# A four-layer spectral mixer on one core: TensorE's waits moved from the head of each unit to the last products of the unit in front

## What is computed

```python
xs = jnp.fft.rfft2(x, axes=(1, 2))                       # 64 x 33 modes
o1 = relu(block_matmul(xs, w1) + b1)                      # 8 blocks of 48 channels, complex
o2 = block_matmul(o1, w2) + b2
out = jnp.fft.irfft2(softshrink(o2, 0.01), s=(64, 64)) + x
```

## Time and profile before

| | |
|---|---|
| median of 3 runs | 995.19 us (990.65 to 997.57) |
| the profiled execution | 993.3 us, of which the span from its first to its last instruction 991.3 us |
| TensorE matmul busy | 916.0 us, 92% |
| VectorE, ScalarE, GpSimd busy | 577.1, 475.8, 81.1 us |
| TensorE's share of the chain that ended last | 82% |
| mean granted clock | 0.976 |

### The profile page before, as it was taken

The page is one execution under the profiler, slowest core; times in us unless marked ns, Lnnn a source line. Parts: engine busy times, 40 slices in busy tenths (PEclk is TensorE's granted clock), DMA queues, the critical chain, the costliest instruction groups (busy, mean ns, idle before and its releaser), DMA issues.

```text
span 991.3 us, 14302 instructions
## 1 busy us (share of the span) xinstructions
PE 916.0 (92%) x5168; PEld 460.3 (46%) x5168; DVE 577.1 (58%) x869; ACT 475.8 (48%) x757; POOL 81.1 (8%) x157
## 2 busy tenths in 40 slices
PE   2799999999999988999999999999999999999933
PEld 1555555665676655444444434444444444444411
DVE  1255555455454765787775676666666666666511
ACT  2455444444545424434343445565655656666521
POOL 3011111011111110000000101000000000000001
PEclk8899999999999999999999999999999999999986
DMA  9879699469648979856143443343654474554463
GB/s 283 324 206 298 202 282 366 150 180 283 248 136 269 260 237 277 210 138 164 48 114 95 112 127 108 108 123 113 213 170 129 153 247 134 161 156 153 142 192 128
DMA packets 95703, 184.41 MB, mean 186 GB/s; under 512 B 13007, under 2 KB 73769, under 8 KB 93842
## 3 DMA queue, kind: packets, MB, share of 16 engines
q1 hardware_dynamic: 85490, 143.65, 48.0%
q0 software_dynamic: 9696, 39.56, 12.4%
q10 hardware_dynamic: 448, 0.30, 0.1%
HBM read 104.32 MB, written 79.14 MB: 185 GB/s over the span
## 4 chain that ended last, share of the span: by engine, by line
PE 82%; DMA 9%; SPq 2%; DVE 2%; ACT 2%; issue 1%; POOL 0%; ACTq 0%; DVEq 0%
PE psum L948 17%; PE psum L957 16%; PE psum L987 8%; PE psum L1041 6%; PE psum L1065 6%; PE psum L1025 6%; DMA RG<-rows_along_h 6%; PE psum L936 5%; PE psum L967 5%; PE psum L998 4%; PE psum L1052 3%; PE psum L913 3%; PE psum L1014 2%; DMA rows_along_h<-RD 1%; SPq L611 1%
## 5 line engine op out<-in xcount | busy, mean ns | idle before, releaser
L1374 DVE SCALAR_TENSOR_TENSOR RA<-psum,RA 112x896 f32<-112x896 f32 (+1 forms) x120 | 124.1, 1035 | 206.3 <-ACT RA L1222 205.9
L1222 ACT ACTIVATE RA<-psum,small 112x896 f32<-112x896 f32 (+1 forms) x120 | 115.7, 964 | 94.7 <-PE psum L957 94.7
L957 PE MATMUL psum<-RA,RW 112*64 112x448 f32 (+1 forms) x640 | 131.1, 531 | 1.4 <-ACT RA L1213 1.4
L1213 ACT ACTIVATE RA<-psum,RW 112x448 f32<-112x448 f32 (+1 forms) x160 | 89.2, 609 | 80.0 <-PE psum L948 80.0
L1334 DVE COPY RD<-psum 128x672 f32<-128x672 f32 (+2 forms) x122 | 69.5, 571 | 58.3 <-PE psum L987 56.8
L987 PE MATMUL psum<-RD,const 128*128 128x384 f32 (+1 forms) x304 | 98.3, 445 | 3.7 <-DVE RD L1334 2.7
L1207 ACT ACTIVATE RA<-psum 128x384 f32<-128x384 f32 (+2 forms) x72 | 50.6, 702 | 78.9 <-PE psum L936 52.6
L936 PE MATMUL psum<-const,RX 128*112 128x128 f32 x528 | 68.5, 282 | 17.1 <-DMA RX<-rows_along_w 17.1
L1359 DVE TENSOR_TENSOR RX<-RX,RA 112x768 f32<-112x768 f32 (+2 forms) x80 | 80.8, 1011 | 2.5
L1207 ACT ACTIVATE RD<-psum 128x384 f32<-128x384 f32 (+2 forms) x122 | 64.0, 525 | 32.9 <-PE psum L987 30.9
L936 PEld LDWEIGHTS psum<-const,RX 128*112 128x112 f32 x528 | 61.2, 180 | 35.7 <-issue 34.9
(11 more groups left out here) (103 smaller groups left out, 1070.1 us busy)
## 6 DMA issues: line engine op xcount, KB each, us to landing
RG<-rows_along_h SPq DMA_DIRECT2D x7, 3072.0 KB, 11.5
RX<-x SPq DMA_DIRECT2D x16, 768.0 KB, 8.6
rows_along_w<-RX SPq DMA_DIRECT2D x54, 224.0 KB, 5.1
rows_along_h<-RD SPq DMA_DIRECT2D x84, 144.0 KB, 3.3
rows_along_h<-RD SPq DMA_DIRECT2D x56, 168.0 KB, 2.9
out<-RA POOLq DMA_DIRECT2D x12, 768.0 KB, 4.0
RX<-rows_along_w SPq DMA_DIRECT2D x12, 672.0 KB, 6.5
spectrum<-RA POOLq DMA_DIRECT2D x48, 168.0 KB, 4.7
```

The source lines that it names most:

```text
L957: mm = nc.tensor.matmul(bank[b * HALF:(b + 1) * HALF, a * BANK:a * BANK + nk * H], w4[layer][0:ROWS, g, b, a], hidden(slot)[0:ROWS, b * N: ...
L1213: done = nc.scalar.activation(hidden(slot)[0:ROWS, b * N:b * N + nk * H], banks(key)[0:ROWS, b, 0:nk * H], ACT.Relu, bias=bias[layer][0:RO ...
L1222: nc.scalar.activation(dst, src, ACT.Relu, bias=minus_lambda_l0 if key[0] == "S4" else minus_lambda).then_inc(act_emptied, 1)
L1374: nc.vector.scalar_tensor_tensor(out=dst, in0=src, scalar=LAMBDA / 64 if key[0] == "S4" else LAMBDA, in1=dst, op0=ALU.add, op1=ALU.min).th ...
```

## The change

The waits are gathered in `ready(key)`, which holds for each kind of unit the same waits as before, with the same values, and the wait for the PSUM slot. `next_ready(key)` calls it for the unit that follows in the order, and each unit's function calls `next_ready(key)` inside its own loop: before its last half (S1, 6C, the mixes, H1, H2, 5A, 5C), before its last two matmuls (S2, 6A, PR, the transposes) or before its last matmul (CF, CI). Seven units and the first keep their waits at their head, for they wait for the very unit in front of them or come after it in a way that would lock. No matmul, order, buffer, DMA or semaphore is changed, and the other engines' programs stay as they are.

```diff
+NOT_AHEAD = {("S2", 0), ("H2", 0, 0), ("H2", 0, 1), ("H2", 1, 1), ("4L2", 0), ("5C", ALL_GROUPS - 1, 0), ("6C", PASSES - 1, 0)}
...
-            def take(key):
+            def ready(key):
+                stage = key[0]
+                if stage == "S1":
+                    _, p, v = key
+                    if v % 2 == 0:
+                        pe.wait_ge(x_loaded[v // 2], 16 * (p + 1))
...
+                elif stage in ("5A", "5C"):
+                    _, e, part = key
...
+                    if part == 0:
+                        for s in (PASS_PAIRS * e, PASS_PAIRS * e + 1):
+                            wait_emptied(pe, ("TA" if stage == "5A" else "TC", s))
...
+                elif stage == "4L3":
+                    wait_emptied(pe, ("3L3", key[1]))
...
                 at = plan.unit[key]
                 if at >= UNITS:
                     wait_emptied(pe, plan.order[at - UNITS])
-                return unit(key)
+
+            def next_ready(key):
+                at = plan.unit[key] + 1
+                if at < len(plan.order) and plan.order[at] not in NOT_AHEAD:
+                    ready(plan.order[at])
 
             def s1(p, v):
                 key, k = ("S1", p, v), v // 2
-                if v % 2 == 0:
-                    pe.wait_ge(x_loaded[k], 16 * (p + 1))
-                bank = take(key)
+                bank = unit(key)
                 n = 2 * PASS_C
                 for to in range(2):
+                    if to == 1:
+                        next_ready(key)
...
-            def mix_second(key, layer, n, slot, first):
+            def mix_second(key, layer, n, slot):
                 _, g, _, nk = step_of(n)
-                bank = take(key)
-                wait_emptied(pe, first)
+                bank = unit(key)
                 for a in range(2):
+                    if a == 1:
+                        next_ready(key)
...
             pe.wait_ge(dft_w_loaded, 16)
             for key in plan.order:
                 stage = key[0]
+                if key == plan.order[0] or key in NOT_AHEAD:
+                    ready(key)
```

More of the change, by code:

```diff
@@ L964, in turn @@
                 nk = step_of(n)[3]
-                bank = take(key)
+                bank = unit(key)
                 for k in range(nk):
+                    if k == nk - 2:
+                        next_ready(key)
                     mm = nc.tensor.transpose(bank[:, k * P:k * P + ROWS], src[0:ROWS, k * P:(k + 1) * P],
@@ L969, in turn, with s5 @@
                 mm.then_inc(filled, 1)
-            def s5(key, matrix, stage, first):
+            def s5(key, matrix, first):
                 _, e, part = key
[L973 to L976, removed]
+                bank = unit(key)
                 for half in range(2):
+                    if half == 1:
+                        next_ready(key)
                     lo, hi = bank_columns(e, part, half)
@@ L991, in s6a @@
                 _, p, g, v = key
-                if g == 0 and v == 0:
-                    pe.wait_ge(g_loaded[p % 2], g_uses(p))
-                bank = take(key)
+                bank = unit(key)
                 n, cols = 2 * KW, slice(g * PASS_C // 2, (g + 1) * PASS_C // 2)
                 for k in range(FLIP_HP):
+                    if k == FLIP_HP - 2:
+                        next_ready(key)
                     at = k // (FLIP_HP // 2) * BANK + k % (FLIP_HP // 2) * n
@@ L1003, in s6c @@
                 _, p, v = key
-                if v == 0:
-                    pe.wait_ge(g_loaded[p % 2], g_uses(PASSES + p))
-                bank = take(key)
+                bank = unit(key)
                 n, k = 2 * PASS_C, v // 2
@@ L1019, in cf @@
                 n = GROUPS[q] * H
-                bank = take(key)
-                pe.wait_ge(y_joined, 2 * (z + 1))
+                bank = unit(key)
                 for part in range(2):
                     for t in range(2):
+                        if part == 1 and t == 1:
+                            next_ready(key)
                         rows = slice(0, FOLD_ROWS + t)
@@ L1031, in h1 @@
                 n = GROUPS[q] * H
[L1032 to L1037, removed]
+                bank = unit(key)
                 for s, src in enumerate((kf[b][:, g], an[b][g // PASS_PAIRS][:, g % PASS_PAIRS])):
+                    if s == 1:
+                        next_ready(key)
                     for r in range(2):
@@ L1047, in h2 @@
                 n = GROUPS[q] * H
-                wait_emptied(pe, ("H1", z, 2 * h + 1))
-                bank = take(key)
+                bank = unit(key)
                 for half in range(2):
+                    if half == 1:
+                        next_ready(key)
                     for r in range(2):
@@ L1059, in ci @@
                 n = GROUPS[q] * H
-                bank = take(key)
-                pe.wait_ge(s_joined, 2 * (z + 1))
+                bank = unit(key)
                 cols = slice(h * FOLD_ROWS, (h + 1) * FOLD_ROWS + h)
@@ L1064, in ci @@
                     for g in range(2):
+                        if part == 1 and g == 1:
+                            next_ready(key)
                         mm = nc.tensor.matmul(bank[0:FOLD_ROWS + h, part * BANK:part * BANK + n],
```

112 lines of the change are left out of this document (74 added, 38 removed).

## The result

The changed kernel takes 1031.89 us (median of 4 runs, 1027.8 to 1033.6) against 996.38 us for the kernel before (4 runs, 990.65 to 998.52). The ratio is 1.0357 with a 95% interval of 1.0327 to 1.0387: slower by 35.5 us. The forecast was 1034 us, in a range of 1013 to 1046.

What follows compares the result with a forecast made beforehand. TensorE was taken as the bound in the long stretches; five terms of late waits sum to 44.3 us, less 5 gives 39, added to the profiled 993.3 us and 1.9 us for the median: 1034 us, range 1013 to 1046.

Steps and rivals of the forecast that it cites:

- Satisfied waits, gain 0: At unit heads on TensorE: a wait long satisfied costs nothing, as eight 6A units run unbroken, so moving it gains 0.
- the rival with chance 0.10: At 495 shape-changing borders: the 0.18 us price is the wait's and all comes back, 945 us; chance 0.10.
- The border's 0.18 us: At 495 of 636 borders, where tile shape changes: about 0.18 us each, put down to shape and left unchanged.
- Terms 1 and 5: Term 1: 4L3 directly behind 4L2, 20 holds, 11.6 us slower; term 5: 25 single cases, 8.9 us slower.
- Term 3: Units behind an S1 or a 6C, 16 late: two of four parallel products held, 11.2 us slower.
- Term 2: 5C behind 3L2, 19 of 35 late: 3L2's last half held for copies, 7.2 us slower.
- The small case of 0.35 us: 5C behind 3L2, waiting for ScalarE's copy of TC: held 0.35 us there; fifteen such, 4.2 us together.
- The four large ones: 5C behind 3L2, four waiting for VectorE's copy of a 6C: 0.71 to 0.81 us each, 3.0 us together.
- Term 4: Nine waits late already, for a DMA or a long VectorE queue: held work runs behind them, 5.4 us slower.
- the 5 us taken off: Off the 44.3 us sum, because holds let ScalarE and VectorE catch up before the next wait; leaves 39 us.
- The rival of parted products: In S1 and 6C: even a satisfied wait parts four parallel products, 41 us more, 1075 us; chance 0.04.
- the four signs: ReLUs between 4L2's halves; 6A's records about 11.1 us; S3 to next start 1.69 us; busy sum unchanged, idle up 40 us.

## Why the prediction was right, point by point

**The bound.** TensorE bounds the long stretches, and every hold is felt at the end: the starts of the last units differ by 39.9 us, the sum of the differences at the borders, and the spans by the same.

**Satisfied waits, gain 0.** Shown by the kernel with 525 waits ahead at the time of before, and by 6A's 11.09 us. The likeliest way to be wrong was the rival with chance 0.10, that the price of a border is the wait's. It rested on the fact that no border between shapes was without a wait. The experiment made 417 of these; they cost what they did.

**The border's 0.18 us.** Put down to the shape, shown with no wait near; a grouped order gave back 0.17 us a change. Only inside 6A is it smaller, 0.12 us.

**Terms 1 and 5** were measured at 11.4 and 9.8 us against 11.6 and 8.9. That term 1 does not shrink was argued from where its ReLUs begin; the trace shows the same 0.57 us with the holds of the whole run behind it.

**Term 3** was too large, 11.2 against 9.1. The size of a hold was right: six S3 behind an S1 lost 0.79 or 0.80 us each, where 0.8 was worked out, and five units behind a 6C 0.55 to 0.80. But some borders that were near the limit lost 0 to 0.2, and behind the first S1 units 0.5 us came back.

**Term 2** was too small, 7.2 against 9.0. The small case of 0.35 us measured 0.44: 3L2 to 5C is 1.92 us and was 1.48. The four large ones measured 0.85 to 0.95 against 0.71 to 0.81. The step that was short is the restart. The held pair starts some 0.1 us after the copy has ended (749.81 against 749.70), which is all I had allowed. But its weights of 112 columns are loaded behind the wait, and so its first pass takes 0.38 to 0.41 us to the next in place of 0.32: some 0.09 us more. In the second mixes, with 64 columns, the start came 0.05 us after the ReLU and the first pass took 0.43 in place of 0.38, so that 0.1 was enough for both.

**Term 4** was far too large, 5.4 against 0.6, and it is where most of the 5 us taken off belong. The 6C of the earlier trace rows shows the reason (timeline of the kernel before, then of the changed one):

```profile
715.98 1.51 PE L957 MATMUL psum<-RA,RW 112*64 112x384 f32 x8
...
720.01 0.88 PE L1014 MATMUL psum<-RG,const 64*64 64x384 f32 x8 [2.51 <-DMA RG<-rows_along_h]
```

```profile
742.53 0.87 PE L1031 MATMUL psum<-RA,RW 112*64 112x384 f32 x4
...
744.64 0.87 PE L1031 MATMUL psum<-RA,RW 112*64 112x384 f32 x4 [1.25 <-DMA RG<-rows_along_h]
...
745.44 0.21 PEld L1089 LDWEIGHTS psum<-RG,const 64*64 64x64 f32 x8 [0.60 <-issue]
```

4L2 starts 26.5 us later than before (742.53 against 715.98), the 6C only 25.4 us (745.44 against 720.01). The held half does cost its 0.8 us. But the DMA did not run later by all that TensorE was late. The load that waits for its data starts 24.6 us later (744.64 against 720.00), nearly what TensorE was late at the last 5C that feeds it, 24.5 us by the unit starts. The 2 us that TensorE lost in between were taken up by the wait. Such a wait is a buffer for losses in front of it; I had counted it as a place of loss alone. At three of the four borders of term 4 that waited for a DMA the distance shrank, by 0.7 to 1.6 us; two 6A that waited for VectorE lost 0.8 and 1.1 us.

**The 5 us taken off** were an estimate that no row gave. Taken alone the terms are 44.3, and measured they are 39.9: terms 3 and 4 came out 2.1 and 4.8 us below what was worked out, terms 2 and 5 came out 1.8 and 0.9 above. That the total came within 1 us is in part luck. By the medians of the runs the change cost 35.5 us, 3.5 less than the 39.

**The rival of parted products** (chance 0.04) did not come: where the wait is satisfied, S1's eight records of a unit still take 0.88 us. Where it is late they do part, and that is term 3.

**What was to be seen.** Three of the four signs stand in the trace: the ReLU between the two halves of 4L2, 6A at 11.09 us, and S3's distance to the next start, as it was wherever the next unit's wait is not late. The fourth came out otherwise. I expected the busy sum to stay and the idle time to grow by some 40 us, and busy time took 26.1 of the growth and idle time 13.8. The record of a held product is longer than its slot, and in an S1 the held products no longer run beside the others; I had not reckoned with either. In the view of waits the loads of the second mix that ScalarE's ReLUs released waited 16.1 us in 32 loads over the whole run before (11.1 us in 21 loads from 580 to 950 us); it is now 24.2 us in 21 loads over the whole run (here the first row):

```profile
PEld psum L1031 <- ACT RA L1269: 24.2, 21, 2.0
...
PEld psum L1021 <- ACT RD L1263: 14.4, 17, 1.5
```

The second row is the hold of 3L2 for TC's copy. L1021 does not read that copy; in the earlier trace rows the copy released 5C, L987, itself.

## What to carry to other kernels

A wait belongs as late in its engine's program as the data allows: on TensorE a satisfied wait costs nothing where it stands, so in this kernel moving it ahead could only hold work that did not need it. To price such a move, compare at each border when the awaited work ends with when the held work could have started, and take the held work's time slot, not its share of the products, as the price. What does cost at a border, 0.1 to 0.2 us, is the change of tile shape, and some of it is won back with the order of the units, as long as the DMAs that hang on that order are moved along.

## What the runs showed of the hardware that was not expected

Holding one of two products that run side by side costs as much as holding both (ratio 1.0361 against 1.0357; at one 4L2 with its 4L3, 3.73 us against 3.74, where 3.16 is the time without a hold).

Matmuls on different parts of the array need not start in the order of the program. In the kernel with the wait before the last product, a pass of 4L3's first product (RN, 612.02) starts before a pass of 4L2's last (RW, 612.22), which the program has in front of it; they stand on different column halves. It is so at all 20 borders of 4L3 behind 4L2 in that kernel.
